# A branch prefetch hint at the top of every engine loop of a graph-network layer

## What is computed

```python
edge_index = jnp.stack([src, dst])
xn = _layernorm(x, axis=-1)
x = x + _L0_gnn_ref(xn, edge_index, ...) + _L0_mix_ref(xn[None], ...)[0]
x = x + _L0_ffn_ref(_layernorm(x, axis=-1)[None], ...)[0]

# _L0_gnn_ref: graph attention, 4 heads of 64, over 200000 edges sorted by dst, plus a loop for each node
e = jax.nn.leaky_relu(a_src[src] + a_dst[dst], 0.2)
m = jax.ops.segment_max(e, dst, num_segments=n)
ex = jnp.exp(e - m[dst])
out = jax.ops.segment_sum(h[src] * (ex / denom[dst])[..., None], dst, num_segments=n)
# _L0_mix_ref: linear attention, 8 heads of 32, between two RMS norms
kv = jnp.einsum('bnhd,bnhm->bhdm', k, v)
# _L0_ffn_ref: 8 experts, each 256 -> 512 -> 256 with a GELU, the best 2 for a row, weighted
h = jax.nn.gelu(jnp.einsum('bsd,dh->bsh', xn, W1[e]) + b1[e], approximate=False)
```

## Time and profile before

| | |
|---|---|
| device time, median of 3 executions | 5643.91 us (5628.12 to 5650.48) |
| the profiled execution's own time | 5658.8 us |
| its span, first to last instruction | 5656.9 us |
| granted TensorE clock, mean | 0.742 of full speed |
| busy: PE / weight loads / DVE / ACT / POOL | 56% / 45% / 49% / 21% / 46% of the span |

### The profile page before, as it was taken

How to read it: one execution, slowest core, us unless ns; L and a number is a source line. 1 busy time by engine, 2 the same in 40 slices (tenths; PEclk the granted TensorE clock), 3 DMA queues, 4 the chain that set the end, 5 groups by cost and what they waited for, 6 DMA issues and landing times. The chain is left out here.

```text
span 5656.9 us, 82461 instructions
## 1 busy us (share of the span) xinstructions
PE 3141.8 (56%) x17248; PEld 2519.1 (45%) x17249; DVE 2765.0 (49%) x6991; ACT 1170.5 (21%) x3323; POOL 2594.0 (46%) x2690
## 2 busy tenths in 40 slices
PE   4997055455555555555566655540034300599998
PEld 3775034343344444444444544430023200599998
DVE  6554234344444444444555677778832400255554
ACT  2443011111111111111111211113322100133332
POOL 3000166666666666666666422224400066444444
PEclk9998577777777777777777766665555555799999
DMA  4111743434344343333333333333311143344443
GB/s 134 57 57 56 223 111 105 105 102 107 103 105 108 101 107 101 104 97 103 102 103 105 87 93 90 93 91 121 122 45 37 41 163 115 86 71 70 71 71 59
DMA packets 414267, 540.74 MB, mean 96 GB/s; under 512 B 70588, under 2 KB 355212, under 8 KB 414078
## 3 DMA queue, kind: packets, MB, share of 16 engines
q0 software_dynamic: 114496, 265.49, 19.2%
q1 hardware_dynamic: 252014, 226.39, 14.4%
q10 hardware_dynamic: 47728, 48.55, 2.6%
HBM read 395.58 MB, written 145.82 MB: 96 GB/s over the span
## 5 line engine op out<-in xcount | busy, mean ns | idle before, releaser
L996 POOL DMA_INDIRECT rows<-node_rows,index x1564 | 1656.7, 1059 | 928.7 <-issue 467.1
L1135 PE MATMUL ps_sum<-msg,hot 128*128 128x260 f32 x3904 | 1238.1, 472 | 908.4 <-DVE big L1077 742.3
L1135 PEld LDWEIGHTS ps_sum<-msg,hot 128*128 128x128 f32 x3904 | 866.6, 234 | 1075.3 <-issue 603.4
L1068 DVE TENSOR_TENSOR msg<-rows,msg 128x1024 f32<-128x1024 f32 x488 | 600.3, 1230 | 81.8 <-ACT msg L1096 63.8
L1050 DVE TENSOR_REDUCE e<-ps_tgt 128x32 f32<-128x96 f32 x488 | 122.9, 252 | 987.3 <-remote 930.0
L1086 ACT ACTIVATE hot<-ps_hot 128x512 f32<-128x512 bf16 x488 | 291.4, 597 | 1280.3 <-remote 787.1
L1841 POOL DMA_INDIRECT out_dram<-big,x_rows x204 | 352.4, 1727 | 438.4 <-DVE big L1933 390.9
L1867 PEld LDWEIGHTS x_ps_hT<-x_rowsT,x_w_now 128*128 128x128 f32 x3264 | 398.8, 193 | 11.5 <-DVE x_w_now L1911 1.1
L1867 PE MATMUL x_ps_hT<-x_rowsT,x_w_now 128*128 128x128 f32 x3264 | 399.8, 276 | 0.7 <-DVE x_w_now L1911 0.7
L1114 PE MATMUL ps_hot<-ident_h,hotT 128*128 128x128 bf16 x1952 | 217.4, 241 | 308.3 <-DVE hotT L1044 159.5
L1876 PE MATMUL x_ps_out<-w,x_actT 128*128 x1632 | 385.9, 379 | 0.0
(11 more groups left out here) (269 smaller groups left out, 4994.6 us busy)
## 6 DMA issues: line engine op xcount, KB each, us to landing
targets<-dst_row SPq DMA_DIRECT2D x391, 128.0 KB
expert_in<-c_blank ACTq DMA_DIRECT2D x51, 520.0 KB
x_rows<-expert_in SPq DMA_DIRECT2D x204, 130.0 KB
rows<-node_rows,index POOLq DMA_INDIRECT x1564
node_rows<-h_out SPq DMA_DIRECT2D x98, 132.0 KB
h_row<-node_rows SPq DMA_DIRECT2D x98, 132.0 KB
queries<-q_out SPq DMA_DIRECT2D x98, 128.0 KB
q_in<-queries SPq DMA_DIRECT2D x98, 128.0 KB
```

What stands on the lines that cost most here:

```text
L996: g.indirect_dma_start(rows[:, j, k, :], None, s.node_rows, bass.IndirectOffsetOnAxis(ap=index[:, b, j * G + k:j * G + k + 1], axis=0)).th ...
L1068: v.tensor_tensor(m[:, :, 0:D].rearrange("p g (h f) -> p g h f", h=GH), rows[:, bass.ds(here, 1), :, 0:D].rearrange("p j g (h f) -> p (j g ...
L1135: mm = pe.matmul(ps_sum[:, j % 2, 0:SUM], hot[:, j % MSGS, k * P:(k + 1) * P], msg[:, j % MSGS, k, :], start=(k == 0), stop=(k == G - 1))
```

## The change

A helper `loop` makes the same loop with one option more: it puts one instruction, a hint for the prefetch of the branch that closes the loop, first in the body. Every loop of every engine is made with it; there are 45 such places in the built program. Nothing else is edited, and the code is laid out as before but for the added instructions.

```diff
+def loop(eng, first, end, step=1):
+
+    return eng.bass.Fori(first, end, step, engines=[eng.engine], hint_back_edge=True)
...
-    with eng.Fori(0, (count - head) // ring) as i:
+    with loop(eng, 0, (count - head) // ring) as i:
...
-                    with v.Fori(14 * j, 14 * (j + 1) + (j == 6)) as t:
+                    with loop(v, 14 * j, 14 * (j + 1) + (j == 6)) as t:
...
-                with v.Fori(0, TILES - 1, 2) as t0:
+                with loop(v, 0, TILES - 1, 2) as t0:
```

More of the change, by code:

```diff
@@ L270, in _ @@
                 sp.sem_inc(store_free, 2)
-                with sp.Fori(0, TILES - 1, 2) as t0:
+                with loop(sp, 0, TILES - 1, 2) as t0:
                     for u in range(2):
@@ L429, in _ @@
                 copy_rT(0, 0)
-                with act.Fori(0, TILES - 1, 2) as t0:
+                with loop(act, 0, TILES - 1, 2) as t0:
                     for u in range(2):
@@ L457, in _ @@
                 transpose_r(0, 0)
-                with pe.Fori(0, TILES - 1, 2) as t0:
+                with loop(pe, 0, TILES - 1, 2) as t0:
                     for u in range(2):
@@ L624, in _ @@
                 with pe.If(faulty(pe, s, 0) != 0):
-                    with pe.Fori(0, COLS) as c:
+                    with loop(pe, 0, COLS) as c:
                         pe.wait_ge(hot_ready, c + 1)
@@ L972, in _ @@
                     track(m, m, m // RING)
-                with sp.Fori(1, LOOPS) as i:
+                with loop(sp, 1, LOOPS) as i:
                     for m in range(UNROLL):
@@ L1000, in _ @@
                     gather(m, m, 0)
-                with g.Fori(1, LOOPS) as i:
+                with loop(g, 1, LOOPS) as i:
                     for m in range(UNROLL):
@@ L1218, in _ @@
                 g.wait_ge(w_in, 48)
-                with g.Fori(0, TILES - 1, 2) as t0:
+                with loop(g, 0, TILES - 1, 2) as t0:
                     for u in range(2):
@@ L1246, in _ @@
                 tile(1, 0, 1, False)
-                with act.Fori(2, TILES - 1, 2) as t0:
+                with loop(act, 2, TILES - 1, 2) as t0:
                     tile(t0, t0, 0, False)
@@ L1399, in _ @@
                 load(1, 1, P)
-                with sp.Fori(2, TILES - 3, 2) as t0:
+                with loop(sp, 2, TILES - 3, 2) as t0:
                     for u in range(2):
@@ L1608, in _ @@
                 centre(1, 1)
-                with act.Fori(0, TILES - 3, 2) as t0:
+                with loop(act, 0, TILES - 3, 2) as t0:
                     for u in range(2):
```

18 lines of the change are left out of this document (9 added, 9 removed).

## The result

The changed kernel takes 5673.15 us (median of 12 executions, 5653.57 to 5685.3), the kernel before 5643.64 us (12, 5624.67 to 5652.22) beside it: 1.0054 times as long, 95% interval 1.0038 to 1.007, which is 21 to 40 us more. It is slower by just over the 0.5% that I had set as the line. The profiled execution of the changed kernel has an own time of 5657.3 us, at the low end of its twelve, and the profiled one of before (5658.8) lies above all twelve of before. So the spans of the two traces (5655.6 and 5656.9) hide the difference, and I read stage by stage.

The account below looks back on a forecast made before the run. Bound: DVE's sequencer work at back edges that nothing covers, not code fetches. 276 exposed hints (99 statistics, 147 `combine`, `join` and `route`, 30 `attend_edges`) x 0.11 = 30 us on 5643.9 gives 5674 us; range 5640 to 5715.

Parts of the forecast that it names:

- The forecast case: Whole kernel: 276 exposed hints at 0.07 to 0.15 us, 0.11 taken, 30 us more, 5674 us; chance 0.56.
- `combine`: Loop of `combine`: DVE's hint exposed in all 49 turns at 0.11 us each, nothing covering the back edge.
- `join`: Loop of `join`: cover under `bn_stats` used up, so DVE's hint exposed in 49 turns at 0.11 us each.
- No fetches to save: All loops: 29 instruction packets mean back edges fetch no code, so the hint saves nothing or next to nothing.
- What one hint costs: Each exposed turn on DVE: 0.11 us, from neighbouring sequencer instructions at 0.12 us in `combine` and 0.08 us in `route`.
- rival A: Exposed turns: hint nearly free, 0.04 to 0.07 us, 8 to 19 us more, about 5658; chance 0.20.
- rival B: Exposed turns: hint dear, 0.15 us and more, 41 to 55 us, up to 61, about 5692; chance 0.13.
- Statistics: Statistics loops of `project`: hint exposed in all 99 turns at 0.11 us, from 48.23 to 59 us.
- rival C: Exposed back edges: hint readies the branch target and speeds them up, 14 to 44 us less; chance 0.07.
- `route`: Loop of `route`: DVE idle 0.23 us behind a back edge, hint exposed in 49 turns at 0.11 us each.
- `attend_edges`: Its DVE loop: about 30 of 60 turns exposed, 3 us; a length change by tens of microseconds would make the forecast wrong.
- Rival D: Exposed turns: hint starts a fetch each turn and the turn waits, 607 us more, 6250; chance 0.04.

Follow-up runs that it names:

- the unrolled kernel: Against the kernel before, no hints: 99 statistics written out, DVE's loops of `combine` and `route` at 14 tiles a turn; 5622.62 us, ratio 0.9966.
- the kernels with one hint: Against the kernel before: statistics written out, DVE's `combine` and `route` at 14 tiles a turn, a hint only in DVE's `combine` loop; 5247.65 us, ratio 0.9938.
- with `combine` left alone: Against the kernel before, no hints: statistics written out, DVE's `route` at 14 tiles a turn, `combine` still at two; 5268.36 us, ratio 0.9975.

## Why the prediction was right, and where it wasn't

The forecast case happened: 5673.15 us measured, 5674 predicted, slower by just over the line. Part of that is luck, as two terms, `combine` and `join`, were off by 6 and 7 us in opposite directions.

- *No fetches to save.* Right. 28 packets for 29, and the unrolled kernel shows what it would have looked like otherwise: 63, with 3.4 us of idle time at each back edge.
- *What one hint costs*, 0.11 us from neighbours between 0.08 and 0.12. Measured 0.079 in the statistics and 0.08 in `route`: `route`'s idle time, the lower neighbour, was the right row. The 0.12 of `combine` divided 0.37 us evenly by three, though 0.19 of them are the branch alone. Of rival A (0.04 to 0.07) and rival B (0.15 and more) neither is met.
- *Statistics*, 99 x 0.11 = 11 us to 59 us. Measured 9 us: 99 x 0.079 = 8, and the gap of 1.3 us on entering the fifth loop. I had costed what other edits might add at nothing; whether this gap is of that kind isn't shown.
- *`combine`*, 49 x 0.11 = 5 us. Measured 11. What failed is not the hint's own cost: at the same clock and with a branch of 196 ns it comes to 6 us, 4 of later starts and the rest a longer wait for PE. What I had at nothing is that the branch ahead of the hint would change: it took 66 ns more in the changed kernel (256 for 190), and the stage is 11 us longer with it.
- *`join`*, 49 x 0.11 = 5 us. Measured -1.8. The cover wasn't used up by the hint, since the back edge itself got 91 ns shorter; that a loop's branch has more than one price, and that an edit elsewhere changes which, was in none of my cases. It isn't rival C either, as it happens in kernels whose loop has no hint.
- *`route`*, 49 x 0.11 = 5 us. Measured 3.9.
- *`attend_edges`*, 3 us. Its own length changed by 25 us between the two traces, which I had named as a reading that would make me wrong. It got shorter, 2493 us, which lies within the 2487 to 2517 us of the traces without hints there, and the kernel with hints there alone takes 1.0005 [0.9987 to 1.0023] of the time. So that sign says nothing here: I had set it without knowing how much the stage varies by itself.
- *`project`'s main loop, POOL's gathers, `run_experts`, the engines beside DVE* at nothing: all as predicted, by the tile of 4.64 us, the idle time of 0.30 us, PE's 696.46 us of 705, and `combine` at 554.7 us with the hints of the other four engines.
- *Sum.* 9.1 + 10.9 - 1.8 + 3.9 = 22 us by the stages for 27 of mine without `attend_edges`, against a median that is 29.5 us higher [21 to 40]. What is left lies within that interval.
- *Rival C*, the back edge sped up. The short branches got slower by 5 ns with a hint (61 for 56), not faster. *Rival D* would have shown in the packets and did not.

## What to carry to other kernels

A hint for the prefetch of a back edge is worth it only where the back edge fetches: look at the packets on the instruction queues, and for idle time of microseconds behind "issue" at the top of a turn. In a short loop it is one more sequencer instruction, about 0.08 us on DVE in each turn where DVE's sequencer sets the pace. There it pays more to have fewer back edges, until the body gets too long to be held, and then one hint on that engine pays for itself many times over.

An edit can besides change by 0.1 us what a back edge elsewhere costs. Before you put a difference of this size down to the edited loop, look at the time from the branch to the next instruction in every loop.

## What the runs showed of the hardware

- A loop of 373 instructions on DVE fetched code in every turn and waited 3.4 us at the back edge; with a hint of 39 ns it did neither. The loop of `route` with 86 instructions a turn fetched nothing without a hint. Between two back edges the packets come some 28 us apart (3292.0, 3320.6 and 3348.1 us), in turns of 82 us: one packet of 8 KB for about 128 of the 373 instructions, so the body takes three. The Trainium skill (Runtime: NRT & Kernel Launch, Instruction fetch mechanics) says that a taken branch to code outside the two pages that are held has to wait for a fetch, and gives the room as 512 instructions for most engines, in blocks of 16 KiB. The wait is there in the trace, with a body that is smaller than that room, but the packets are of 8 KB; two of those would hold some 256 instructions, fewer than the body. How many are held no run here shows.
- `bn_stats` of 128x256 has a duration of 0.427 us in every row, but 14 of them in a row took 4.67 us, 0.33 us each. The duration of one is no bound for the pace of many; I had used it as one for the unrolled kernel, and the gain was 11 us where I expected 6.
- From DVE's compare-and-branch to its next instruction it is 190 or 287 ns in `combine` and 191, 274, 287 or 309 in `join` without a hint, 196 or 256 in `combine` with one, for the same loop. Of seven loops with one body in one program, six take 191 ns and one 267.
- On the chip of the kernels with one hint and with `combine` left alone, the kernel before is 6.4% faster (5280 us). By the traces of those two, the whole difference lies in `attend_edges`: 2137 and 2139 us from the first to the last `msg` there, 2487 to 2517 on the others; the main loop of `project` (450 us), `join`, `scatter_rows` and `run_experts` (754 us) take what they take elsewhere. The cause was not looked for.
